# A four-part fused kernel: the time-mixing weight is loaded raw during the input matrix, and four smaller moves

## What is computed

```python
x = x + einsum('bct,bcd->bdt', x, W0[ids0])          # a 64x64 channel matrix, picked per batch
x = x + ssm_conv(x, ssm1) masked by len1             # per channel: causal convolution of length 1024
x = x + (x @ w2.T + bias + scale * (x @ A.T) @ B.T)  # over time: w2 is 1024x1024, A/B are LoRA, rank 16
x = x + ssm_conv(x, ssm3) masked by len3
```

## Time and profile before

| | |
|---|---|
| median of three runs | 1708.16 us |
| the profiled execution | 1710.22 us |
| its span, first to last instruction | 1708.2 us |
| PE busy | 1578.8 us (92%) |
| DVE busy | 1029.7 us (60%) |
| ACT busy | 531.8 us (31%) |
| POOL busy | 826.4 us (48%) |
| bytes moved by DMA | 216.80 MB |

### The profile page before, as it was taken

One profiled execution on the slowest core, in us unless ns is written; L12 is line 12 of the kernel. 1 busy time (PEld: TensorE's weight loads), 2 busy tenths in 40 slices (PEclk: granted clock), 3 DMA queues, 4 the chain that ended last, 5 costly groups with the idle time before them and its releaser, 6 DMA issues.

```text
span 1708.2 us, 30846 instructions
## 1 busy us (share of the span) xinstructions
PE 1578.8 (92%) x12183; PEld 1033.3 (60%) x12183; DVE 1029.7 (60%) x1336; ACT 531.8 (31%) x674; POOL 826.4 (48%) x365
## 2 busy tenths in 40 slices
PE   6577774899999999999999999999999999999996
PEld 6576773365666656565657574747474747474744
DVE  6577766546575756565655656665656565656532
ACT  3444442323232323232323232323232323232211
POOL 2000006336556555656565656574747473838334
PEclk9888987899999999999999999999999999999998
DMA  4799994336263535353535252626252525252314
GB/s 120 195 334 368 356 342 159 74 48 160 48 147 60 140 66 135 71 135 71 135 70 136 61 145 52 149 47 148 58 140 66 140 66 140 66 128 74 79 50 99
DMA packets 433122, 216.80 MB, mean 127 GB/s; under 512 B 345336, under 2 KB 419584, under 8 KB 431040
## 3 DMA queue, kind: packets, MB, share of 16 engines
q1 hardware_dynamic: 413760, 204.19, 45.5%
q10 hardware_dynamic: 19328, 12.14, 2.5%
HBM read 94.19 MB, written 71.76 MB: 97 GB/s over the span
## 4 chain that ended last, share of the span: by engine, by line
PE 82%; DVE 6%; DMA 4%; issue 3%; SPq 2%; ACT 2%; ACTq 1%; POOL 0%; POOLq 0%; DVEq 0%
PE ps L730 39%; PE ps L765 7%; PE ps L668 7%; PE ps L695 6%; PE ps L722 5%; PE ps L738 5%; DMA arena<-in_x_dram 4%; PE ps L778 3%; PE ps L612 3%; PE ps L672 3%; PE ps L712 2%; PE ps L708 1%; SPq L352 1%; PE ps L561 1%; DVE arena L1462 1%
## 5 line engine op out<-in xcount | busy, mean ns | idle before, releaser
L730 PE MATMUL ps<-arena,w2t 128*128 128x512 f16 x3072 | 681.3, 379 | 0.0
L730 PEld LDWEIGHTS ps<-arena,w2t 128*128 128x128 f16 x3072 | 300.6, 98 | 362.5
L529 POOL TENSOR_TENSOR arena<-arena 128x1024 f32<-128x1024 f16 x64 | 152.8, 2387 | 545.8 <-DMA arena<-arena 528.2
L1468 DVE TENSOR_SCALAR arena<-ps,biasx 128x512 f32<-128x512 f32 x128 | 94.3, 747 | 214.6 <-ACT arena L1056 214.4
L1056 ACT ACTIVATE arena<-ps,biasx 128x512 f16<-128x512 f32 x128 | 87.3, 688 | 425.6 <-PE ps L738 425.6
L505 POOL TENSOR_TENSOR arena<-arena 128x1024 f32<-128x1024 f32 x32 | 73.7, 2305 | 288.6 <-DMA arena<-tab_scratch 261.3
L612 PE MATMUL ps<-arena 128*128 128x128 f32 x1024 | 150.2, 312 | 57.5 <-DMA arena<-in_x_dram 35.9
L612 PEld LDWEIGHTS ps<-arena 128*128 128x128 f32 x1024 | 141.3, 223 | 64.8 <-issue 33.8
L695 PE MATMUL ps<-arena 128*128 128x512 f16 (+1 forms) x768 | 138.7, 332 | 11.8 <-DVE arena L1389 9.4
L765 PE MATMUL ps<-arena 128*128 128x256 f16 (+1 forms) x1536 | 138.8, 247 | 3.2 <-DVE arena L1462 3.0
L532 POOL TENSOR_TENSOR arena<-arena,one_xs 128x1024 f32<-128x1024 f32 x64 | 136.1, 2126 | 5.0
(11 more groups left out here) (211 smaller groups left out, 2126.8 us busy)
## 6 DMA issues: line engine op xcount, KB each, us to landing
arena<-in_x_dram SPq DMA_DIRECT2D x64, 512.0 KB, 8.9
out_dram<-arena SPq DMA_DIRECT2D x64, 512.0 KB, 2.9
gbuf<-x_scratch SPq DMA_DIRECT2D x120, 256.0 KB, 3.6
x_scratch<-arena SPq DMA_DIRECT2D x16, 1024.0 KB, 11.6
arena<-krow_scratch SPq DMA_DIRECT2D x32, 512.0 KB, 4.4
x_scratch<-arena SPq DMA_DIRECT2D x16, 896.0 KB, 8.8
arena<-tab_scratch SPq DMA_DIRECT2D x32, 200.0 KB, 2.7
gbuf<-in_L_cond_weight_dram ACTq DMA_DIRECT2D x8, 512.0 KB, 8.4
```

The source lines that it names most:

```text
L529: nc.gpsimd.tensor_tensor(past[:, h % 2].rearrange("p (k t) -> p k t", k=NBLK), x3t[:, h % 2, 0], x3t[:, h % 2, 1], ALU.add).then_inc(past ...
L730: nc.tensor.matmul(ps[:, 4 + o % 3, :], w2t[:, part, k, o * P:(o + 1) * P], xx[:, :, k, :], start=(k == 0 and q == 0), stop=False)
L1468: ts(x3f[:, o % 2], ps[:, 4 + o % 3, :].rearrange("p (h b) -> p h b", h=HG), XS / FS, biasx[:, o:o + 1], ALU.mult, ALU.add).then_inc(s2_ou ...
```

## The change

- `w2t` gets the layout (block of outputs, half, k, output), so that the 4 KB of one output block hold either its two float16 halves or 128 raw float32 rows. All eight raw blocks are loaded there by ACT between the `pick` copies (`load_weights`), and LoRA A and B after them (`load_adapters`). The eight loads of w2 at L851 go out of their places. In stage 0 DVE copies a raw block to a row buffer (`lot_ready`, a `tensor_scalar` of 1024 elements), then as before.
- LoRA B is loaded to `lora_raw` in runs of 512 B instead of 64 B and permuted by DVE (`lora_rows`); its halves are written to `bt` contiguously, read strided from PSUM.
- The lots are turned in another order: A and B in unit 0, w2 blocks 0 and 1 in unit 1, then one in each unit.
- `adapter_scales` is one instruction in unit 1; what doesn't need the loads goes into the parameter chain.
- `combine_b` moves from the end of its unit to behind the first `copy_odd` of the next, `store_tab` one step on; for the last chunk, `combine_b`, `store_tab`, `sum_k`, `scale_k`, `split_k` and `store_k` go into the turn, behind the work of group 0.
- The stores of a unit are issued at steps 6, 7, 8, 9 instead of 6, 8, 10, 12. In the turn the transposes of the bases go ahead of the last unit's stores, and SP waits for fewer of the kernel and table stores.
- The split of group 1's x1 moves into body 0, behind outputs 4 to 7 of `stage2`.

```diff
-        w2t = sb("w2t", [P, 2, NBLK, T], F16)
+        w2t = sb("w2t", [P, NBLK, 2, NBLK, P], F16)
...
-        wrow = [part_of(gbuf, 32 + 4 * r, 4) for r in range(2)]
+        lrow = [part_of(gbuf, 32 + 4 * r, 4) for r in range(2)]
+        lora_raw = part_of(gbuf, 8, 4)
+        wrow = w2t[:, :, :, :, :].rearrange("p n s k o -> p n (s k o)").bitcast(F32)
...
-        LOT_A, LOT_W0, LOT_B, LOT_W = 0, 1, 2, 2
+        LOT_A, LOT_B, LOT_W = 0, 1, 2
...
             if isinstance(n, int) and n == LOT_B:
-                return bt[:, part, :].rearrange("p (o j) -> p j o", j=NBLK)
+                return bt[:, part, :].rearrange("p (o j) -> p o j", j=NBLK)
...
-            return w2t[:, part, :, bass.ds(weight_block(n) * P, P)]
+            return w2t[:, bass.ds(n - LOT_W, 1), part].rearrange("p n k o -> p (n k) o")
...
-            return ps[:, 6:8, :].rearrange("p q (m o) -> p (q m) o", m=4)
+            tiles = ps[:, 6:8, :].rearrange("p q (m o) -> p (q m) o", m=4)
+            return tiles.rearrange("p m o -> p o m") if isinstance(n, int) and n == LOT_B else tiles
...
-            STORE_AT = {6: 0, 8: 1, 10: 2, 12: 3}
+            STORE_AT = {6: 0, 7: 1, 8: 2, 9: 3}
...
             load_g(0, 0)
+            wait_u(0, 0)
+            turn_u(0, 0)
             for part in range(NPART):
                 store_x1(NBLK // 2 - 1, 1, part)
-            for part in range(NPART):
-                sp.wait_ge(x1_stored[0][part], 16 * NBLK // 2)
-            wait_u(0, 0)
-            turn_u(0, 0)
-            sp.wait_ge(krow_stored, 16 + 32 * NBLK)
-            for r in range(2):
-                sp.wait_ge(tab_stored[r], 16 * NBLK // 2)
+            sp.wait_ge(krow_stored, 16 + 32 * (NBLK // 2 + 1))
+            sp.wait_ge(tab_stored[0], 16 * (NBLK // 4 + 1))
             load_g(1, 0)
             load_tab(1, 0)
+            sp.wait_ge(v_lo, 1)
             load_tab(0, 1)
             for part in range(NPART):
                 sp.wait_ge(x1_stored[1][part], 16 * NBLK // 2)
...
+                if isinstance(g, int) and g == 0:
+                    sp.wait_ge(krow_stored, 16 + 32 * NBLK)
+                    for r in range(2):
+                        sp.wait_ge(tab_stored[r], 16 * NBLK // 2)
...
                         if step == 5:
-                            turn_lot(LOT_W0)
+                            turn_lot(LOT_B)
                     else:
                         if step == 1:
                             sum_k(blk - 1)
                         if first and step == 3:
-                            turn_lot(LOT_B)
-                        if step == 5:
+                            turn_lot(LOT_W)
+                        if first and step == 6:
+                            turn_lot(LOT_W + 1)
+                        if not first and step == 5:
                             turn_lot(blk + LOT_W, k)
...
-            sum_k(NBLK - 1)
...
-                            nc.tensor.matmul(ps[:, 4 + o % 3, :], w2t[:, part, k, o * P:(o + 1) * P], xx[:, :, k, :],
+                            nc.tensor.matmul(ps[:, 4 + o % 3, :], w2t[:, o, part, k, :], xx[:, :, k, :],
...
                 if h >= 2:
                     near1(0, h)
                 far1(0, h)
+            sum_k(NBLK - 1)
             pe.wait_ge(k_scaled, NBLK)
...
+            def load_weights(n):
+                act.dma_start(wrow[:, n], w2[n * P:(n + 1) * P, :]).then_inc(wrow_loaded, 16)
+
+            def load_adapters():
+                act.dma_start(lrow[LOT_A], lora_a.rearrange("a r i -> (a r) i")).then_inc(lrow_loaded[LOT_A], 16)
+                act.dma_start(lora_raw.rearrange("p (a n) -> p a n", a=NADAPT),
+                              lora_b.rearrange("a (p m) r -> p a (m r)", m=NBLK)).then_inc(lrow_loaded[LOT_B], 16)
...
-            load_lot(LOT_A)
-            load_lot(LOT_W0)
...
                     e = nc.scalar.activation(pick[rows, :, q * C + 8 * dgroup:q * C + 8 * dgroup + 8],
                                              ps[rows, dgroup, :].rearrange("p (e n) -> p n e", e=8), ACT.Copy, scale=FS)
                 e.then_inc(pick_copied, 1)
+                load_weights(dgroup)
+            load_adapters()
...
                         if step == 6:
-                            lot_hi(LOT_W0)
-                            load_lot(LOT_B)
-                            load_lot(LOT_W + 1, 0, 1)
+                            lot_hi(LOT_B)
                     else:
-                        if step == 0:
+                        if step == 1:
                             store_tab(blk - 1, 1 - k)
-                            if not (first and k == 1):
-                                load_lot(blk + LOT_W, i, k)
                         if step == 2:
                             scale_k(blk - 1)
                         if first and step == 4:
-                            lot_hi(LOT_B)
+                            lot_hi(LOT_W)
+                        if first and step == 7:
+                            lot_hi(LOT_W + 1)
+                        if not first and step == 6:
+                            lot_hi(blk + LOT_W)
                         if step == 7:
                             store_k(blk - 1)
-                            lot_hi(blk + LOT_W)
                     chunk_sines(blk, k, step)
...
             for h in range(HG):
                 x1_split_hi(0, h)
             bases_hi(0, 0)
-            store_tab(NBLK - 1, 1)
-            scale_k(NBLK - 1)
             table_hi(0, 0)
-            store_k(NBLK - 1)
             act.wait_ge(tab_stored[0], 16 * NBLK // 2)
             for k in range(NCH - 1):
                 state_hi(0, 0, k)
+            store_tab(NBLK - 1, 1)
             for h in range(HG):
                 x2_split_hi(0, h)
-            for h in range(HG):
-                x1_split_hi(1, h)
+            scale_k(NBLK - 1)
+            store_k(NBLK - 1)
             act.wait_ge(tab_stored[1], 16 * NBLK // 2)
...
                                          bias=biasx[:, o:o + 1], scale=XS / FS).then_inc(x3_hi, 1)
+                    if isinstance(g, int) and g == 0 and o >= HG:
+                        x1_split_hi(1, o - HG)
                     if more1 and o == 1:
...
+            link(ts(rank_adapter, pcol, 1.0 / RANK, -0.5 + 0.5 / RANK, ALU.mult, ALU.add))
+            link(ts(rank_adapter, rank_adapter, ROUND, ROUND, ALU.add, ALU.subtract))
+            ts(adapter_scale[:, :], idf[:, 2, :], rank_adapter, None, ALU.is_equal)
             link(ts(quarter_own, pcol, float(C), 0.25, ALU.is_lt, ALU.mult))
...
             def adapter_scales():
 
                 dve.wait_ge(consts_loaded, 16 * NADAPT)
-                link(ts(rank_adapter, pcol, 1.0 / RANK, -0.5 + 0.5 / RANK, ALU.mult, ALU.add))
-                link(ts(rank_adapter, rank_adapter, ROUND, ROUND, ALU.add, ALU.subtract))
-                link(ts(rank_scale, rank_scale, XS / FS, None, ALU.mult))
-                ts(adapter_scale[:, :], idf[:, 2, :], rank_adapter, rank_scale, ALU.is_equal, ALU.mult)
+                ts(adapter_scale[:, :], adapter_scale[:, :], rank_scale, XS / FS, ALU.mult, ALU.mult)
...
+            def lot_ready(n, parity=None):
+
+                if isinstance(n, int) and n == LOT_W:
+                    dve.wait_ge(wrow_loaded, 16 * NBLK)
+                dve.wait_ge(w2_turned, n - 1)
+                row = row_of(n, parity)
+                ts(row, wrow[:, bass.ds(n - LOT_W, 1)].rearrange("p n i -> p (n i)"), 1.0, None, ALU.mult).then_inc(w2_copied, 1)
+                dve.wait_ge(w2_copied, n - LOT_W + 1)
+                own = row[:, bass.ds((n - LOT_W) * P, P)]
                 tt(own, own, ident[:, :], ALU.add).then_inc(w2_ready, 1)
+
+            def lora_rows():
+                dve.wait_ge(lrow_loaded[LOT_B], 16)
+                nc.vector.tensor_copy(lrow[LOT_B].rearrange("p (m a r) -> p a m r", m=NBLK, a=NADAPT),
+                                      lora_raw.rearrange("p (a m r) -> p a m r", a=NADAPT, m=NBLK)).then_inc(lora_ready, 1)
...
                         if step == 1:
                             turned_bias()
                         if step == 4:
-                            lot_ready(LOT_W0, 0, 1)
+                            lora_rows()
                         if step == 5:
                             lot_lo(LOT_A)
+                        if step == 7:
+                            lot_lo(LOT_B)
+                    else:
+                        if step == 0:
+                            combine_b(blk - 1, 1 - k)
+                        if first and step == 2:
+                            lot_ready(LOT_W)
+                        if first and step == 4:
                             adapter_scales()
-                        if step == 7:
-                            lot_lo(LOT_W0)
-                    else:
-                        if step == 1 and not (first and blk == 1):
-                            lot_lo(blk - 1 + LOT_W)
                         if first and step == 5:
-                            lot_lo(LOT_B)
```

(22 more changed lines are left out.)

37 lines of the change are left out of this document (11 added, 26 removed).

## The result

The kernel after takes **1717.1 us** (median of 5 runs, 1715.5 to 1718.3), the kernel before beside it 1708.6 us (5 runs, 1705.7 to 1711.7): a ratio of 1.005, 95% interval 1.0039 to 1.0062. It is slower by half a per cent, where 27 us less were forecast. The profiled spans, 1715.2 and 1708.2 us, differ by 7.0 us, the medians by 8.5.

A forecast was written before the change was run, and what follows sets the result against it. The prediction took DMA to bound stage 0's units, a chain the turn, and PE fifteen of sixteen bodies. Its terms, -17.3 - 2.0 - 8.4 - 3.5 + 4.3 = -26.9 us, gave 1681 us, range 1668 to 1695.

The forecast's parts named there:

- part 3: Stage 0 units: six w2 blocks leave the DMA-bound units at 1.4 us each, 8.4 us earlier, bounds 0 and 8.9.
- The earlier stores move no bytes: Stage 0 units: four stores in a row may idle DMA up to 1 us a unit, or gain as much; net nothing.
- B: Stage 0: freed bytes become idle time, units stay at 26 us, collision with POOL whole; 1693 us, chance 0.22.
- rival E: Body 0: PE's stand sets its clock to 0.50 through two convolutions; slower, 1716 us, chance 0.04.
- Part 1: Unit 0: no stand for the scales, combine_b no longer ahead; first store 17.3 us earlier at 56.0, bounds 13 and 19.
- Parts 2 and 3: Stage 0: cheaper LoRA B halves in unit 0, 2.0 us earlier; w2 traffic out of DMA-bound units, 8.4 us earlier.
- rival D: Unit 0: early loads miss DMA's idle time and meet the tiles, first store some 6 us later; 1687 us, chance 0.07.
- Part 4: The turn: combine_b leaves the stretch behind the last sum; net 3.5 us earlier, bounds 8.3 and -1.
- the collision with POOL: Turn: most moves to combine_a, 5 of 8.1 us return; if combine_a and keep_x1 were met wholly, turn gives 1.8 us.
- the term for POOL's next table: Turn: SP's v_lo wait delays only this load, landing about 31 us after the last sum as before; no cost.
- Part 5: Body 0: split behind output 7 makes PE stand 3.3 us, plus a slower clock; 4.3 us later, bounds 3.3 and 6.5.

The follow-up runs named there:

- a_both: Kernel after with the stores back at steps 6, 8, 10, 12 and the split of group 1's x1 back ahead of body 0: 1680.1 us.
- b_scale: Kernel before with only the last step of the adapter scales, which needs the tiny loads, moved from unit 0 to unit 1: 1702.8 us.
- a_comb: a_both with combine_b back at the end of its own unit, the last one too: 1693.6 us.
- a_store: Kernel after with only the stores of a unit back at steps 6, 8, 10, 12: 1685.8 us.
- a_late: a_both with w2 blocks 2 to 7 loaded at the start of their units in stage 0 again: 1687.7 us.
- a_gate: a_both with POOL's second table loaded only when the last x2 split of group 0 is done: 1676.7 us.
- a_split: Kernel after with only the split of group 1's x1 back ahead of body 0: 1711.8 us.
- a_warm: Kernel after with two batches of 12 unused identity products on PE in each stage 0 unit but the first, ahead of awaited tiles: 1702.3 us.
- b_store: Kernel before with only the stores of a unit moved to steps 6, 7, 8, 9: 1751.9 us.
- a_runs64: a_both with LoRA B loaded in 64 B runs again, at its new early place, and copied plainly by lora_rows: 1684.3 us.

## Why the prediction was wrong

**The step that failed** is in part 3: "The earlier stores move no bytes", with the price "I take nothing for both, and keep -6 and +6 us". The order of bytes had a price: 31.3 us in the total, 31.8 in the units (202.8 against 171.0), measured by undoing just that: the stores keep the tiles away, PE stands and its granted clock falls, and then DMA stands behind the slow PE. I had seen both halves of the mechanism (four stores in a row, a PE slower than DMA afterwards) and set it at up to 1 us a unit, without working out how long PE gets no tile. The trace of before was enough for an estimate: four parts are 3.9 MB (two of 1024 and two of 896 KB in the page's DMA issues), and at 355 GB/s that is 11 us, against four loaded tiles that PE works off in 8.2, which leaves a stand of some 3 us in each unit; and a stand of 4.54 us had been followed by a half clock. I used these rows for body 0 in rival E and not in stage 0, where they tell more: at half clock a tile takes 3.8 us (measured in after), and the eight tiles of a unit would take 30, more than DMA's 26.

**The rivals.** B had the mechanism in half a sentence ("bursts of stores") and the wrong size: it ended at 1693 us, with units of 26 us, while they came out at 27.8 to 29.8. E had the right side and the right time (1716) by the wrong place: the clock in body 0 stayed at 0.96 on the mean (it was at 0.50 from 370 to 372 us, behind the stand, and at 1.00 from 374), and most of its 4.6 us is the stand, as in the forecast. The nearness of its time is chance. a_both at 1680.1 isn't the forecast come true either, as it isn't the kernel that was predicted.

**Part 1** held: the first store at 54.87 instead of the forecast 56.0. Its pieces have their own measurements: the wait for the scales 12.7 us (b_scale, where the halves of LoRA B were still dear), `combine_b` ahead of the store 4.3 (a_comb) against 3.9.

**Parts 2 and 3** without the stores: -12.0 us in the units of a_store, against the forecast -10.4. w2's six blocks are 7.6 us in the total (a_late) against 8.4, but 5.5 in the stretch where the forecast had them. The loads at their early place are no burden: in the page of after the eight blocks land 3.4 us after their issue (8.4 before):

```profile
w2t<-in_L_cond_weight_dram ACTq DMA_DIRECT2D x8, 512.0 KB, 3.4
```

So rival D had no ground.

**Part 4** was wrong by 4.3 us, -3.5 against +0.8 (+0.5 in a_both, where the stores of the units play no part). The first thing that failed: I counted the collision with POOL as met by one group of instructions, `combine_a`, and for a part only, and expected the rest to come back. In the kernel after itself `combine_a` is met in full:

```profile
252.12 1.93 POOL L508 TENSOR_TENSOR arena<-arena 128x1024 f32<-128x1024 f32 x1 [242.10 <-DMA arena<-tab_scratch]
253.02 1.32 DVE L1264 TENSOR_TENSOR arena<-arena,gbuf 128x256 f32<-128x256 f32 x1
...
258.94 2.05 DVE L1267 TENSOR_TENSOR arena<-arena,gbuf 128x272 f32<-128x272 f32 x1
```

In a_both `combine_a` escapes, and `x1_split_lo` pays instead. Whatever instruction of this kind stands beside POOL's here, it gets some 1.6 us longer: 2.05 instead of 0.44, 2.8 on the mean instead of 1.22. Moving one group out of the way brings the next one in. The Trainium skill, page "SBUF — State Buffer", section "SBUF: two separate sides", says that the pair of ports is taken for the whole of an instruction, and names instructions of VectorE with two inputs in SBUF, beside GpSimd instructions that read SBUF, among those it holds for. The rows above agree in so far as the whole group is met. With `combine_a` met in full the forecast had -1.8 for the turn, which is nearer than my -3.5 but still on the wrong side, because it too was applied to two groups alone.

The second thing that failed is the term for POOL's next table, which was to land "about 31 us after the last sum as before". In before POOL began the second table 30.6 us behind the last sum (256.25) and was through with it 8 us before the turn's end; in after it begins 38.6 us behind the last sum (257.66) and lies beside `x2_split_lo` until `stage2` starts at 311.90:

```profile
286.88 1.93 POOL L505 TENSOR_TENSOR arena<-arena 128x1024 f32<-128x1024 f32 x1 [16.31 <-DMA arena<-tab_scratch]
...
300.26 1.05 POOL L519 TENSOR_TENSOR arena<-twin,arena 128x512 f32<-128x512 f32 x1
```

```profile
296.28 1.93 POOL L508 TENSOR_TENSOR arena<-arena 128x1024 f32<-128x1024 f32 x1 [30.02 <-DMA arena<-tab_scratch]
...
310.63 2.04 POOL L522 TENSOR_TENSOR arena<-twin,arena 128x512 f32<-128x512 f32 x1
```

(The first fence is POOL's timeline of before, the second that of after.) In before two of the four `x2_split_lo` met it (2.76 and 1.96 us, the others 1.22 and 1.23), in after three (2.84, 2.94 and 2.96 us): some 2.8 us more. Added to -1.8 this gives +1.0, against +0.8 measured. I had asked who waits for the load, and not whom POOL would then stand beside.

Why did the load land late? Not by the new wait for `v_lo`. SP's issues, of before and then of after (L352 and L354 the last unit's stores, L375 and L377 the loads of two tables), and the instruction of after that `v_lo` stands for:

```profile
264.90 3.11 SPq L352 DMA_DIRECT2D x_scratch<-arena  x4
280.58 1.06 SPq L375 DMA_DIRECT2D arena<-tab_scratch  x2
```

```profile
278.91 3.34 SPq L354 DMA_DIRECT2D x_scratch<-arena  x4
283.60 6.26 SPq L377 DMA_DIRECT2D arena<-tab_scratch  x2
```

```profile
275.98 1.75 DVE L1408 SCALAR_TENSOR_TENSOR arena<-arena 128x1536 f16<-128x1536 f32 x1
```

The wait was over at 277.73, before SP came to the loads. What changed is what they stand behind: the four stores of 3.9 MB went out 15.7 us ahead of them in before and 4.7 us in after, since the transposes now go first. POOL began 6.3 us behind the issue of the first of the two loads in before, 12.7 in after and 12.8 in a_both. That the stores hold them up is argued from these times; no run puts them back. If so, it is the step of part 3 once more: large stores just ahead of a load that something waits for, priced at nothing. With the second table out of the way (a_gate) the turn is 4.7 us shorter than before, which is the forecast's side and about its size.

**Part 5** held: +4.6 against +4.3, and by a_split 4.1 in body 0. PE's wait is 3.46 us, against 3.3; for the low clock behind it the forecast took 1 us, and PE was busy 0.9 us longer than in a_split (89.97 against 89.12). In the total the split costs 5.3 to 5.7 us, so 1 us more than body 0 shows; where it lies is open.

**What stays open.** How the 22 us that a_warm leaves in the units divide between the slots, the added work and what is left of the low clock (0.94 in the unit shown). Why the same edit costs 43 us in the kernel before and 31 in after: 37.8 against 31.8 in the units, and 7.5 more in the turn of b_store, where a_store and after have the same turn. The w2 blocks in the bursts of before would lengthen them, but that was only argued. In a_gate the last sum came 4.5 us later than in a_both (230.27 and 225.75), though its edit lies behind it; the profiled execution was the slowest of its four, 2.4 us above their median, so one execution doesn't tell such a difference. The turn's length varies between 48.8 and 60.9 us over the kernels of the table, and only a part of that is explained here.

## What to carry to other kernels

Where an engine lives on small loads in few slots, the order of the large stores between them is a cost of its own, even if not a byte changes: work out for how long a burst of stores keeps the next load away, against the work that the slots hold, and spread them. A share of DMA below 1.00 in a stretch that DMA bounded before, with waits for loads (here 2.8 to 6.7 us) and a half clock behind them, is the sign of it. And before two-input work of VectorE is moved out of GpSimd's way, look at what moves in: the saving is what the whole chain meets, not what one group does. When a large transfer is moved behind something urgent, look at what it now stands ahead of.

## What the runs showed of the hardware

- Work added to PE in its waits made the kernel 15 us faster (a_warm); the tile behind it took 2.05 us at a granted clock of 1.00, instead of 3.78 at 0.50.
- VectorE instructions with two inputs in SBUF took some 1.6 us longer beside POOL's: 2.05 instead of 0.44 us, 2.8 instead of 1.22. A wait that holds POOL's work back past the chain gave the turn 5.2 us (a_gate).
- With two loads of 200 KB issued 4.7 us behind 3.9 MB of stores, POOL, which needed one of them, began 12.7 us behind the first issue (after), and 6.3 where the stores were 15.7 us ahead (before).
- With the stores spread over the unit DMA moved 391 GB/s for 21 us, where the unit shown of before has 355.
- The stores' order alone moved the rate of stage 0 from 350 (64.0 MB in 183.0 us, before) to 290 GB/s (b_store).
- An issue behind a load in runs of 64 B took 9.15 us at 31.56 us, as it had taken 8.50 at another place, and 0.60 us behind the same load in runs of 512 B: the price goes with the short runs, not with the place. While it lasted the DMA share was over 1.00 in both, at 155 GB/s (36.00 to 40.70 us of a_runs64) and 143 (56.00 to 60.10 us of before).
